# Two-layer graph network: a quarter of the opening on GpSimd, turned weights rounded earlier, and 38 extra TensorE multiplications

## The reference

```python
h = relu(layernorm(x))
x = x + (adj @ (h @ weight) + bias)            # layer 0
h = relu(layernorm(x))
for _ in range(5):                             # layer 1
    m = adj @ h
    av = concat([m, m])
    u3 = h @ u3_w.T + u3_b
    z = sigmoid(av @ w3_w.T + w3_b + u3)
    r = sigmoid(av @ w4_w.T + w4_b + u3)
    hv = tanh(av @ w5_w.T + w5_b + (r * h @ u5_w.T + u5_b))
    h = (1 - z) * h + z * hv
x = x + h
```

## Time and profile before

| | |
|---|---|
| median of 3 runs | 1474.78 us (1474.74 to 1474.79) |
| the profiled execution | 1475.47 us, its span 1473.5 us |
| TensorE busy | 1445.2 us, 98% |
| VectorE busy | 1232.7 us, 84% |
| ScalarE busy | 937.0 us, 64% |
| GpSimd busy | 209.2 us, 14% |
| mean granted TensorE clock | 0.999 |

### The profile page before, as it was taken

How to read it: one execution, slowest core, us unless ns; L and a number is a source line. 1 busy time by engine, 2 the same in 40 slices (tenths; PEclk the granted TensorE clock), 3 DMA queues, 4 the chain that set the end, 5 groups by cost and what they waited for, 6 DMA issues and landing times.

```text
span 1473.5 us, 20135 instructions
## 1 busy us (share of the span) xinstructions
PE 1445.2 (98%) x7017; PEld 676.6 (46%) x7017; DVE 1232.7 (84%) x1718; ACT 937.0 (64%) x1448; POOL 209.2 (14%) x392
## 2 busy tenths in 40 slices
PE   5899999999999999999999999999999999999999
PEld 4553444444444444444444444444444444444444
DVE  7889788888788888888778978889778888887778
ACT  4556656667568565776566666676665865566654
POOL 3440003310230004040203000413021100000000
PEclk9999999999999999999999999999999999999999
DMA  5513424371533323554432343347164232243322
GB/s 190 58 29 57 99 53 82 58 94 33 77 82 58 79 58 61 125 73 72 58 58 57 62 97 65 73 96 87 40 80 86 44 62 54 55 89 65 68 55 86
DMA packets 333171, 105.83 MB, mean 72 GB/s; under 512 B 310416, under 2 KB 327696, under 8 KB 333072
## 3 DMA queue, kind: packets, MB, share of 16 engines
q1 hardware_dynamic: 315696, 95.56, 31.7%
q0 software_dynamic: 16512, 8.39, 5.7%
q10 hardware_dynamic: 864, 0.59, 0.1%
HBM read 13.24 MB, written 8.39 MB: 15 GB/s over the span
## 4 chain that ended last, share of the span: by engine, by line
PE 88%; DVE 5%; ACT 1%; issue 1%; DVEq 0%
PE ps_a L706 30%; PE ps_c L706 15%; PE ps_b L706 7%; PE ps_u L793 7%; PE ps_u L797 7%; PE ps_u L795 7%; PE ps_v L793 4%; PE ps_v L795 4%; PE ps_v L797 4%; DVE rh L1483 1%; DVE rh L1479 1%; DVE h_lo L1490 1%; DVE area L1458 1%; DVE nx_lo L1435 0%; DVE rh L1466 0%
## 5 line engine op out<-in xcount | busy, mean ns | idle before, releaser
L706 PE MATMUL ps_a<-t_hi,nx_hi 128*128 128x512 f16 x576 | 218.3, 379 | 1.2 <-ACT rh L1059 1.2
L706 PE MATMUL ps_a<-t_lo,nx_hi 128*128 128x512 f16 x576 | 218.3, 379 | 0.0
L706 PE MATMUL ps_a<-t_hi,nx_lo 128*128 128x512 f16 x576 | 218.3, 379 | 0.0
L1077 ACT ACTIVATE rh<-ps_v,bias,w_inv 128x512 f32<-128x512 f32 x160 | 123.8, 777 | 84.5 <-PE ps_v L797 84.5
L1073 ACT ACTIVATE m_hi<-rh 128x512 f16<-128x512 f32 x138 | 86.4, 628 | 111.8 <-DVE rh L1466 111.4
L1518 DVE TENSOR_TENSOR rh<-rh,area 128x512 f32<-128x512 f32 x160 | 109.6, 696 | 54.3 <-ACT rh L1082 50.7
L1059 ACT ACTIVATE rh<-ps_a 128x512 f32<-128x512 f32 x138 | 81.3, 589 | 108.9 <-PE ps_a L706 100.8
L1082 ACT ACTIVATE rh<-ps_u,bias,w_inv 128x512 f32<-128x512 f32 x160 | 120.0, 773 | 20.8 <-PE ps_u L797 19.2
L1090 ACT ACTIVATE area<-ps_u,bias,w_inv 128x512 f32<-128x512 f32 x160 | 121.9, 770 | 16.9 <-PE ps_u L797 16.9
L1479 DVE SCALAR_TENSOR_TENSOR rh<-rh,area 128x1024 f32<-128x1024 f32 x78 | 95.3, 1222 | 44.0 <-ACT rh L1077 43.6
L1522 DVE TENSOR_TENSOR rh_lo<-rh,rh_hi 128x512 f16<-128x512 f32 x160 | 109.7, 687 | 20.1 <-ACT rh_hi L1095 17.8
(11 more groups left out here) (246 smaller groups left out, 3162.9 us busy)
## 6 DMA issues: line engine op xcount, KB each, us to landing
xr<-b_rows POOLq DMA_DIRECT2D x6, 1024.0 KB, 14.0
xr<-in_x_dram SPq DMA_DIRECT2D x5, 1024.0 KB, 5.7
out_dram<-xr SPq DMA_DIRECT2D x5, 1024.0 KB, 4.2
area<-in_adj_dram SPq DMA_DIRECT2D x8, 512.0 KB, 7.6
nx_hi<-s SPq DMA_TRANSPOSE x128, 2.4
nx_lo<-s SPq DMA_TRANSPOSE x128, 2.5
area<-in_x_dram SPq DMA_DIRECT2D x2, 1024.0 KB, 5.5
area<-b_rows POOLq DMA_DIRECT2D x2, 1024.0 KB, 13.4
```

What stands on the lines that cost most here:

```text
L706: last = nc.tensor.matmul(o[:, :], a[:, PLACE[k], j, :], b[:, k, j, :], start=(opens and j == 0 and n == 0), stop=(j == HB - 1 and n == 2) ...
L1077: nc.scalar.activation(cand[:, q, :], V_BANK[q][:, :], ACT.Tanh, bias=bias[:, BV:BV + 1], scale=w_inv[:, CAND:CAND + 1]).then_inc(cand_rea ...
```

## The change

It has four parts, all in the opening of group 0.

1. TensorE: ten multiplications of `ones` with `ident` (128 x 128, fp32) into a bank that nobody reads before it is overwritten, after units 0 to 4 have been turned, and 28 more after the spread, before the first `direct_product`. They wait for nothing.
2. GpSimd: quarter 3 of slot 0 is normalised here (four scalings and a maximum) and not on ScalarE, between the moments of batch 1 and those of slot 1. `bias_x(0, 0)` is moved ahead of slot 1's moments.
3. ScalarE: quarter 3's normalising is gone, quarter 2's is put ahead of `round_unit(11)`.
4. ScalarE and VectorE: the turned weights and `round_m(g, 3)`/`rest_m(g, 3)` are moved ahead of slot 1's second batch, on ScalarE between its quarters 2 and 3, on VectorE ahead of the difference K_S3.

```diff
+    AWAKE = (10, 28)
+            def normalise_fourth():
+
+                pool.wait_ge(moment_op[0], MOMENT_OPS)
+                for b in range(3 * HB, 4 * HB):
+                    last = nc.gpsimd.tensor_scalar(ysc[:, b, :], xr[0][:, b, :], rstd[0][:, b:b + 1],
+                                                   shift[0][:, b:b + 1], ALU.mult, ALU.add)
+                last.then_inc(y_fourth_op, 1)
+                pool.wait_ge(y_fourth_op, 1)
+                nc.gpsimd.tensor_scalar(ysc[:, 3 * HB:4 * HB, :], ysc[:, 3 * HB:4 * HB, :], 0.0, None, ALU.max
+                                        ).then_inc(y_ready[0], 1)
+
             moments(pool, 0, 0, 0, slice(0, 1), first_moment_op, stats_first)
             moments(pool, 0, 0, 0, slice(1, 2))
+            normalise_fourth()
+            bias_x(0, 0)
             moments(pool, 0, 0, 1)
-            bias_x(0, 0)
             scale_weights()
...
+            def stay_awake(count):
+                for _ in range(count):
+                    nc.tensor.matmul(ps_b[:, 0:P], ones[:, :], ident[:, :], start=True, stop=True)
...
                     for unit in range(len(ps_adj)):
                         transpose_unit(unit)
+                    stay_awake(AWAKE[0])
                     pe.wait_ge(top_op, 3)
                     pe.wait_ge(w0_top_op, 3)
                     nc.tensor.matmul(ps_c[:, 0:P], ones[:, :], top_diag[:, 0, :], start=True, stop=True
                                      ).then_inc(top_spread, 1)
+                    stay_awake(AWAKE[1])
                     direct_product(0, 0, range(len(ps_adj), len(ps_adj) + 2 * HB))
...
-                    for unit in range(3 * HB):
+                    for unit in range(3 * HB - 1):
                         round_unit(unit)
                     normalise(0, 0, 0, range(2, 3))
+                    round_unit(3 * HB - 1)
                     round_rows(K_S4)
-                    normalise(0, 0, 0, range(3, 4))
                     round_n(0, 0, 0, 1)
...
-                    normalise(0, 0, 1, range(2, 4))
+                    normalise(0, 0, 1, range(2, 3))
+                    round_turned_weights()
+                    round_m(g, 3)
+                    normalise(0, 0, 1, range(3, 4))
                     round_n(0, 0, 1, 1)
-                    round_m(g, 3)
-                    round_turned_weights()
...
+                    rest_turned_weights()
+                    rest_m(g, 3)
                     sum_rows(K_S3)
                     rest_n(0, 0, 1, 1)
-                    rest_m(g, 3)
-                    rest_turned_weights()
```

More of the change, by code:

```diff
@@ L243, in gnn_kernel @@
         y_late_op = sem("y_late_op")
+        y_fourth_op = sem("y_fourth_op")
         c_done = sem("c_done")
```

## The result

The changed kernel takes 1479.38 us (median of 8 runs, 1479.08 to 1480.42), the kernel before in the same sessions 1474.97 us (8 runs, 1472.80 to 1475.93). The ratio is 1.0030, 95% interval 1.0020 to 1.0039: slower by 4.4 us. The profiled execution took 1479.22 us with a span of 1477.3 us, which is 3.8 us more than the span of before.

The account below looks back on a forecast made before the run. TensorE, busy 98% of the span, was taken as the bound: +0.3 us by 40.75, +4.15 by unit 21, +2.8 by 86.68, giving 1477.5 from a median of 1474.78. Range 1473.3 to 1480.0; the forecast's own 1476.3 to 1479.3.

Parts of the forecast that it names:

- slower: Whole kernel: a time more than about 0.2% above the kernel before, beyond 1477.7 us; chance 0.34.
- within: Whole kernel: a change of no more than about 0.2%, 2.9 us, either way; chance 0.57.
- the first rival: Opening on TensorE: transposes count, clock rises at 14.4 to 15.5, the ten delay nothing; about 1476.0 us; chance 0.27.
- the DMA's issue: GpSimd ahead of slot 1's chain: bias DMA 0.3 us, then 1.43 until the next instruction, bound above 2.27.
- the clock's fall: Behind the new 3.8 us idle before unit 21: costs 0 to 1.7 us, half taken, +0.9.
- The 38 multiplications: Opening on TensorE: ten slow, 28 at 0.22 us; first product at 25.3 against 20.94, TensorE 2.0 us later in it.
- the ten end at 18.7, the spread is 1.6 us late: TensorE after the opening transposes: ten multiplications run at the low clock and delay the spread from 17.09 by 1.6 us.
- The quarter on GpSimd: Opening: ScalarE loses 1.6 us, third product only +0.3; GpSimd pays 3.1 plus the DMA, slot 1's chain starts at 36.4.
- The chain: GpSimd's slot 1 moments, blocked by VectorE's differences, end at about 48.9 instead of 43.94.
- Unit 21: Its transposes on TensorE start at 55.9 instead of 51.75, after 3.8 us of new idle time.
- Turned weights first: Before layer_out: the 2.05 us wait goes, but x1 starts 4.6 later, at 69.6, so TensorE can't use the gain.
- The sum: Whole opening: +2.8 us, from +0.3 by 40.75, +4.15 by unit 21 and +2.8 by 86.68.

Follow-up runs that it names:

- e4: The kernel before with only the turned weights and slot 0's last m moved ahead of slot 1's second batch: 1472.75 us, ratio 0.9987.
- e1: The changed kernel without its 38 multiplications, the rest of the change kept: 1479.32 us, ratio 1.0028 to the kernel before.
- e6: The changed kernel with the bias DMA behind slot 1's moments and 10 and 14 multiplications instead of 10 and 28: 1475.39 us, ratio 1.0007.
- e7: The kernel before with the turned weights moved and 10 and 14 multiplications, the quarter still on ScalarE: 1471.31 us, ratio 0.9978.
- e9: The changed kernel with 19 more unread multiplications in TensorE's wait before unit 21: 1476.92 us, ratio 1.0011 to the kernel before.
- e5: The kernel before with the quarter on GpSimd and the bias DMA ahead of slot 1's moments, no multiplications, weights in their old place: 1480.25 us, ratio 1.0039.
- after: The changed kernel with all four parts, against the kernel before: 1479.38 us, ratio 1.0030.
- e3: The changed kernel with slot 0's bias DMA put back behind slot 1's moments, the quarter staying on GpSimd: 1473.91 us, ratio 0.9993.
- e2: The kernel before with only the 38 multiplications added: 1476.53 us, ratio 1.0009.

## Why the prediction was right, and where it was wrong

The forecast was 1477.5 us, the time is 1479.4, inside the range and above the bound of "slower", to which I had given 0.34 against 0.57 for "within". The cause that I named, GpSimd's chain and the idle time before unit 21, is the one that the runs show.

That the number is so near is partly luck. The condition of the first rival came true, and for it I had 1476.0 (1475 to 1477.5), which is 3.4 us too little. What the early clock saved was made up by terms that were too small: 1.2 us in the DMA's issue, 0.8 in the clock's fall, and 0.75 at the kernel's end that I did not have at all. These leave 0.6 us.

- **The 38 multiplications.** The step "the ten end at 18.7, the spread is 1.6 us late" failed. The first rival was right here: the ten ran fast, and transposes can raise the clock. In e4 TensorE does nothing but the twenty transposes between 9.90 and the spread at 16.99, and this took 0.49 us (the one multiplication before them, at 6.96, ended 2.2 us ahead of them). In the profile of before it was slow (0.80), and I took that for the rule; but in e1, whose last eight transposes already took 1.54 us instead of 1.91, the clock was up at 13.6 and down again at 17.0, in the wait before the spread, which then took 0.80. A slow instruction behind an idle stretch doesn't tell that the work before it left the clock down. What the Trainium skill says in "TensorE: Matmul & The Clock Gate", Part 4: PE-mode transpose, that the full clock doesn't engage for them, doesn't hold for these fp32 transposes, and the measurement decides. When it rises differs from run to run: in e6, e7 and e9 the ten took 3.0 to 3.2 us, so the first of them were still slow, but the spread came at 17.23 to 17.29 there too. The 28 and the first product (25.3 forecast, 23.8 measured) differ by the same error.
- **The quarter on GpSimd.** Four scalings 1.75 as reckoned, the maximum 1.49 for 1.4. Under-sized was the DMA: 0.65 and 2.28 us instead of 0.3 and 1.43. The next instruction's start is no measure of when GpSimd is free.
- **The chain.** 48.9 forecast, 48.27 measured: too much from the ten, too little from the DMA, and these two made up for each other. The last difference caught it, as reckoned, but the sum has a slip: of the 3.45 us that remained at 42.8, 1.05 were left at 46.0 and not 0.5.
- **Unit 21.** 55.9 forecast, 55.38 measured.
- **Turned weights first.** The old wait is gone, and the gain is not collected because x1 is late: x1 at 69.6 forecast (70.5 with the clock's 0.9), 70.41 measured. The slack behind it was 2.4 us, 2.7 forecast (the 0.8 of it is 0.69 by its own rows). By itself this part is worth 2.2 us (e4).
- **The clock's fall.** I took half of 1.7 us; e9 shows 1.7, and e1 and e5 1.8 to 2.4. So the bound of 1.7 in my range was too low. In `after`, unit 21 is the first instruction behind the wait, and the clock fell 0.2 us after it began, so that no part of the slow stretch lay in the wait.
- **The sum.** +2.8 forecast by 86.68, +3.0 measured. Not in it: the 0.75 us at the end, which came in the kernels with 38 multiplications and in no other. Together 3.8 in the profiled executions; the medians are 4.4 apart, and the 0.6 between is not explained beyond the spread of the runs of before.

Settled: the order of the bias DMA and slot 1's moments is the loss (5.5 us, e3), not the 38 (e1; by the kernel's end their two effects of 1.2 and 0.75 us nearly cancel). Left open: that the packet on the instruction queue loads TensorE's own instructions, and that it is what slows SyncE's issue. That rests on the two standing together in the traces; neither was changed by itself.

## What to carry to other kernels

An engine with little to do may still hold the chain that everybody waits for: before work is put ahead of such a chain, see who is released by its last step, and what blocks it if it comes later. Idle multiplications that keep the clock up pay where they fit in a wait (10 and 14 in the opening: 1.4 us between e4 and e7; 19 in the wait of e9: 1.7 us) and cost what sticks out of it (14 more: 3.1 us). Price such parts alone and together, since here the same edit was worth 2.2 us in one order and 0.9 in the other.

## What the hardware showed that I had not expected

- The clock was raised by transposes alone: in e4 the twenty from 9.90 to 14.40 ran slow, and the next instruction, at 16.99, ran at the full clock (0.49 us). In before, e1 and e5 the same instruction took 0.80.
- A wait of 2.05 us (2.04 in e2) was followed by a fall of the clock in before's profile and by none in those of e2 and e5. In e2 the mean clocks of the runs (1.000 or 0.998 to 0.999) go with two groups of times some 1.5 us apart.
- A DMA issue on GpSimd of 2.28 us lets the next instruction show a start 1.45 us after its own, but that instruction then takes 1.11 us instead of 0.23.
- A GpSimd step of 0.2 us took up to 2.37 us beside VectorE's TENSOR_TENSOR on 128x2048 (2.28 us). The chain of moments, 23 operations by the rows of the trace, took 6.75 us in its half-wide form and 10.4 in its full one, where three operations took 1.22, 2.15 and 0.59 us beside VectorE's.
- An issue of SyncE took up to 2.21 us instead of 1.27 beside a packet of the instruction queue, in the kernels with 38 multiplications, and at the kernel's end that is 0.75 us of their time. The cause is not shown.
